# First stage of a two-layer decoder: the third pair of hidden products moves to the keys' PSUM bank, and the receptance's sigmoid stays in PSUM

## The reference, cut to what matters

```
h = layernorm(x) * g + b;  hh = h shifted by one token
k = (h mixed with hh by tm_k) @ Wk.T ;  v, r likewise with Wv, Wr
sr = sigmoid(r)                                    # the receptance
rwkv = sr * wkv(k, v)                              # a scan over the tokens, with exponentials
x1 = x + rwkv @ Wo.T
g = layernorm(x1) ...; gk, gr = g mixed with g shifted
kf = square(relu(gk @ Fk.T))                       # 1024 hidden channels
x2 = x1 + sigmoid(gr @ Fr.T) * (kf @ Fv.T)         # the channel mix
```

## Time and profile before

| | |
|---|---|
| median of the runs | 2665.17 us (2663.54 to 2668.63) |
| the profiled execution | 2672.59 us, its span 2670.9 us |
| busy over the span | PE 91%, DVE 70%, ACT 43%, POOL 38% |
| first stage | from the start to 463.2 us, where the next stage's first product starts |
| steady part of it | one half takes 25.4 us |

### The profile page before, as it was taken

One profiled execution on the slowest core, in us unless ns is written; L12 is line 12 of the kernel. 1 busy time (PEld: TensorE's weight loads), 2 busy tenths in 40 slices (PEclk: granted clock), 3 DMA queues, 4 the chain that ended last, 5 costly groups with the idle time before them and its releaser, 6 DMA issues. The chain is left out here.

```text
span 2670.9 us, 52343 instructions
## 1 busy us (share of the span) xinstructions
PE 2418.6 (91%) x18321; PEld 2028.7 (76%) x18321; DVE 1880.6 (70%) x5088; ACT 1138.2 (43%) x2100; POOL 1024.0 (38%) x1429
## 2 busy tenths in 40 slices
PE   3999998899999699999999999997987999996697
PEld 2887787566666499999999999996875666663692
DVE  6999994677777466666776676666866588886465
ACT  2656554465554322222222222222484565663462
POOL 3555554111111165325653354311112145554672
PEclk8999999899998699999999999998988999997799
DMA  3334101324321020002312112103102245320438
GB/s 115 105 110 151 60 1 25 84 71 118 85 65 46 25 96 32 32 28 78 111 32 73 45 58 75 35 30 128 48 13 57 76 116 138 80 73 2 129 95 322
DMA packets 164252, 204.44 MB, mean 77 GB/s; under 512 B 21059, under 2 KB 138350, under 8 KB 164080
## 3 DMA queue, kind: packets, MB, share of 16 engines
q1 hardware_dynamic: 134576, 155.45, 20.0%
q0 software_dynamic: 15648, 23.70, 2.7%
q10 hardware_dynamic: 13856, 23.07, 2.4%
HBM read 95.76 MB, written 75.45 MB: 64 GB/s over the span
## 5 line engine op out<-in xcount | busy, mean ns | idle before, releaser
L2017 PE MATMUL m_gu<-m_x_hi,m_w_hi 128*128 128x256 f32 x1632 | 460.9, 282 | 2.0 <-DVE m_x_lo L2079 2.0
L2017 PE MATMUL m_gu<-m_x_lo,m_w_hi 128*128 128x256 f32 x1632 | 456.1, 279 | 0.0
L2017 PE MATMUL m_gu<-m_x_hi,m_w_lo 128*128 128x256 f32 x1632 | 456.1, 279 | 0.0
L2049 ACT ACTIVATE m_sg<-m_gu 128x256 f32<-128x256 f32 x408 | 156.6, 385 | 654.4 <-PE m_gu L2017 645.8
L2098 DVE TENSOR_TENSOR m_h<-m_sg,m_gu 128x256 f32<-128x256 f32 x408 | 171.2, 420 | 244.5 <-ACT m_sg L2049 233.2
L1402 ACT ACTIVATE x_pt<-x_ps 128x1024 f32<-128x1024 f32 x256 | 262.1, 1024 | 180.0 <-PE x_ps L1147 175.6
L2017 PEld LDWEIGHTS m_gu<-m_x_hi,m_w_hi 128*128 128x128 f32 x1632 | 309.6, 190 | 4.9 <-DVE m_x_lo L2079 2.4
L2017 PEld LDWEIGHTS m_gu<-m_x_lo,m_w_hi 128*128 128x128 f32 x1632 | 308.3, 189 | 0.0
L2017 PEld LDWEIGHTS m_gu<-m_x_hi,m_w_lo 128*128 128x128 f32 x1632 | 307.9, 189 | 0.0
L1533 DVE CUSTOM_DVE_ANT_0 x_ps<-x_ps,c_mb 128x256 f32<-128x256 f32 x512 | 201.4, 455 | 97.0 <-PE x_ps L1147 97.0
L2004 PE MATMUL m_yp<-m_w_hi,m_h_hi 128*128 128x256 f32 x816 | 239.0, 293 | 9.9 <-DVE m_h_lo L2100 8.1
(11 more groups left out here) (377 smaller groups left out, 5522.3 us busy)
## 6 DMA issues: line engine op xcount, KB each, us to landing
yt<-zero SPq DMA_DIRECT2D x8, 2048.0 KB, 10.7
m_yr<-yt SPq DMA_DIRECT2D x16, 1024.0 KB, 17.7
x_kpack<-x_kh SPq DMA_DIRECT2D x120, 128.0 KB
x_qpack<-x_qh SPq DMA_DIRECT2D x120, 128.0 KB
m_x<-xs SPq DMA_DIRECT2D x36, 258.0 KB
xs<-zero SPq DMA_DIRECT2D x8, 1072.0 KB, 6.0
m_x<-xs SPq DMA_DIRECT2D x32, 268.0 KB
c_cx<-in_ctx SPq DMA_DIRECT2D x32, 256.0 KB, 3.2
```

What stands on the lines that cost most here:

```text
L2017: ins = pe.matmul(gu[:, m % 4, n, :], wp[n][:, c, m * P:m * P + P], xp_[:, c, :], start=(c == 0 and k == 0), stop=(c == KC - 1 and k == 2))
L2049: act.activation(sg[:, m % 4, :], gu[:, m % 4, 0, :], ACT.Silu).then_inc(silu_ready, 1)
```

## The change

The third pair goes to bank K instead of R and waits for `new_args` instead of `sr_ready`. The sigmoid is written back into bank R, in place, and VectorE's last product in `numerators` reads it there. The next stage's key projection (and its two readers on ScalarE) goes to bank R instead of K. The SBUF tensor `sr` stays allocated, as it serves the next stage's keys under another name.

```
-    HID = (HID0, HID1, R, HID0)
+    HID = (HID0, HID1, K, HID0)
@@ hidden (TensorE)
                     if j == 2:
-                        pe.wait_ge(sr_ready, min(s + 3, B))
+                        pe.wait_ge(new_args, min(s + 3, B))
@@ cross_keys (TensorE)
-                project(K, cross.wqk[:, 1], cross.cx[:, 0]).then_inc(cross.k_ready, 1)
+                project(R, cross.wqk[:, 1], cross.cx[:, 0]).then_inc(cross.k_ready, 1)
@@ gate (ScalarE)
-                act.activation(sr[:], flat(R), ACT.Sigmoid).then_inc(sr_ready, 1)
+                act.activation(flat(R), flat(R), ACT.Sigmoid).then_inc(sr_ready, 1)
@@ last half (ScalarE)
-                    cross_keep(1, K, cross_kf, cross_kh, cross.k_ready, cross.kh_ready)
+                    cross_keep(1, R, cross_kf, cross_kh, cross.k_ready, cross.kh_ready)
@@ numerators (VectorE)
-                s_.do(dve.tensor_tensor(y1[:], y1[:], sr[:], ALU.mult))
+                s_.do(dve.tensor_tensor(y1[:], y1[:], flat(R), ALU.mult))
```

## The result

The changed kernel takes 2658.6 us (median of 20 runs, 2649.6 to 2674.62), the kernel before 2669.71 us (20 runs, 2661.23 to 2682.99). The ratio is 0.9954, 95% interval 0.994 to 0.9968: 12.3 us faster, 8.5 to 16.0. Two more series of the same kernel against runs of the kernel before on other occasions gave 0.9957 (0.9941 to 0.9973) and 0.9967 (0.9946 to 0.9987). The forecast was 10.1 us.

The account below looks back on a forecast made before the run. VectorE's queue was taken to bound the steady first stage, TensorE the last halves. 9.4 us (13 x 0.72) plus 0.8 gave 10.1 us off 2672.59, 2662.5; shifted to the runs' median, 2655.0 us, range 2652 to 2660.5.

Parts of the forecast that it names:

- the predicted 9.4 + 0.8: First stage: VectorE gains 0.72 us in each of 13 halves, 9.4; TensorE gains 0.77 us once in the last halves.
- the predicted 453.1: Sign: the next stage's first product comes at about 453.1 us in place of 463.2.
- The bound: Steady part of the first stage: VectorE's queue sets the half; TensorE's wait for the sigmoid, 1.78 us, is slack.
- the near end of 0.685: VectorE's product L707 after the change: 0.655 us taken, with 0.628 and 0.685 as near ends, 1.41 as far end.
- The rival of a dearer read: L707 reading PSUM takes 0.748 us, L710 starts at 214.12; total 2655.8 us; chance 0.08.
- The count, 13: Of 16 L707 products, 13 are long (seq 2 to 14) and gain; seq 0, 1 and 15 gain nothing.
- The slower rival: ScalarE's sigmoid write to PSUM waits for TensorE's running matmuls, up to 1.74 us per half; 2679.4 us; chance 0.04.
- the bound of 13 x 0.06 = 0.8 us: ScalarE's sigmoid delay, at most 0.06 us, is passed on one to one through L392 to L710 in 13 halves.
- The new wait for the ReLU: TensorE at L487: the wait on sigmoid L568 goes; one on ReLU L582 of 0.8 to 1.1 us replaces it.
- the gain in the drain: Half 16: TensorE's shorter wait brings 0.77 us once; bounds 0 and 1.78.
- The 0.3 us before the values' last part: Steady half, TensorE: the square of pair 3 on ScalarE makes the values wait some 0.3 us.
- The wait that only moves: L707 is still held by GpSimd, or L710 as long; only the drain's 0.8 us stays, 2664.4 us; chance 0.09.

Follow-up runs that it names:

- the two repeats: The changed kernel, unaltered, profiled and timed again on other occasions; ratios to the kernel before 0.9957 and 0.9967.
- Each part alone: Changed kernel with the sigmoid back in SBUF, 2663.67 us; changed kernel with the third pair still waiting for the sigmoid, 2647.18 us; one run each.
- the shorter difference: Kernel before, with GpSimd's difference L392 computed for one of two channel halves; half 24.94 us, one run 2652.77 us.
- one more ScalarE operation: Changed kernel plus a ScalarE copy of 512 SBUF elements behind the sigmoid in every half; half 24.86 us, one run 2671.02 us.
- the other operand's run: Changed kernel with the sigmoid to SBUF and the sum L705 written to bank R instead; half 24.66 us, one run 2643.91 us.

## Why the prediction was right

The forecast was 10.1 us of gain, the measured ratio says 12.3 (8.5 to 16.0). The time, 2658.6 us, lies 3.6 above the number and in the range; the predicted difference was taken off a median of 3 runs, 2665.17, and 20 runs put the kernel before at 2669.71. Of the 3.6 us, 4.5 come from that base, and the larger difference of the medians (11.1 us) takes 1.0 off. In the steady part and the drain, where scatter is small, the predicted 9.4 + 0.8 stand against a measured 9.5 + 0.74. That the stage ended at 452.07, even before the predicted 453.1, was the luck of an early start; the two repeats ended at 453.26 and 451.21.

- **The bound.** VectorE's queue, not TensorE's. Each part alone shows it: 8.76 us for the operand in PSUM, 0.80 for TensorE's wait.
- **L707.** Its cause was named rightly, by three runs: halving GpSimd's operation shortens it, moving either operand cures it, moving neither leaves it at 1.41. Its new size was off: 0.688 us instead of 0.655, just above the near end of 0.685. The error cost nothing, as L710 was to wait for L392 in any case and starts 0.72 us behind L707, as the prediction has it. With 0.688 the wait at L710 has become a tie: taking the product's own 0.69 off its end puts the release 0.13 to 0.15 us before the recorded end of L392 (214.06 against 214.21 in the kernel before, 209.36 against 209.50 with the shorter difference, 210.19 against 210.32 with one more ScalarE operation), and in the changed kernel L710 starts at 209.46, 0.14 before L392's end at 209.60. The rival of a dearer read had 0.748 for L707 and 0.78 from its start to L710's, against 0.688 and 0.72. The Trainium skill's dearer PSUM source ("VectorE: DVE Perf Modes", section "The TRN2 errata — SBUF-src ops pay a fixed extra latency per instruction") would have made it 0.757; it took 0.688, and 0.691 with both inputs in SBUF. (The prediction's own numbers for that case, 0.65 us in each of 13 halves, give 8.5 us and not 8.6.)
- **The count, 13.** The 12 steps from seq 2 to seq 14 gained 8.75 us, 0.73 each; seq 15 gained nothing.
- **ScalarE.** Taken as 0; it is -0.015 us (582 against 597 ns), worth 0.03 a half at most, by the other operand's run, and by the medians there less. The slower rival, a sigmoid held up by TensorE's writes, is refuted by a spread of 0 ns over 16. The Trainium skill has ScalarE writing to PSUM faster than to SBUF ("ScalarE: Activation LUTs", section "Step-by-step: what each stage is for"); the trace agrees, by 15 ns. That ScalarE's delays pass on through L392 is shown, at 0.22 us for 0.62, but not one to one, as the prediction had it: the first 0.3 us go into L392's wait behind L705, so that the bound of 13 x 0.06 = 0.8 us on the slow side was not there.
- **TensorE.** The new wait for the ReLU is 0.71 to 0.73 us (1.07 in one half) instead of 0.8 to 1.1, and the gain in the drain 0.74 instead of 0.77. The 0.3 us before the values' last part appeared as 0.42 at its weight load; the values take 7.40 us in place of 7.07, so that a half's work on TensorE besides its wait is 23.9 us and not 23.6, which is what the new wait is short.
- **The start of the stage.** Not in the sum, 0.9 us in the first comparison, and within the scatter that the repeats show there.
- **Rivals.** The wait that only moves did not happen here, but only just, as the tie at L710 says: once VectorE came to L710 some 0.6 us sooner, L710 paid 0.29 us. The difference is how long VectorE takes from L705 on against when L392 is released.

## What to carry to other kernels

Compare one operation's shortest and its usual duration before looking at waits: a VectorE operation at twice its shortest, with two inputs, both in SBUF, and a GpSimd operation beside it, was here a wait that no semaphore shows. Moving one of its inputs to PSUM took it away, and the next such operation in line must be checked against the end of the same GpSimd operation. Where totals scatter more than the change is worth, measure from one mark of the steady part to the next stage's first instruction.

## What the runs showed that I had not expected

A single input in SBUF did not wait: the reciprocal L696 (205.60 to 208.95 in the kernel before) lies beside GpSimd's L400 (206.79 to 208.83) and takes 3.35 us in all 16. The scan with one input in PSUM takes 1.222 us against 1.29 us with both in SBUF and no GpSimd beside it; that this is the operand's place is not shown, as the other scan, L692, takes 1.19 to 1.23 us with both inputs in SBUF. GpSimd's L405 is 1.18 us in place of 2.10 once the scan lets it pass: by the order of the rows the scan waited for GpSimd's L403, and L405 for the scan. The first two sequences, with TensorE's granted clock at 0.61 from 35 to 45 us of the profile after and 0.67 in a repeat, take up to 2 us more or less from one execution to the next of one kernel (seq 2's L710 at 85.50 to 87.51 us).
